# Sorted token rows packed without gaps for the expert layers, and the second pool's choices made in two parts

## What is computed

```python
x = x + 0.5 * ffn(layernorm(x))
x = x + attn(layernorm(x), Wqkv, Wo)      # 16 heads, 4 key-value heads, head size 128, causal, rotary
x = x + 0.5 * ffn(layernorm(x))

def ffn(x):                               # 16 experts, 2 per token, inner size 96
    probs = softmax(x @ router_w)
    weight, chosen = top_k(probs, 2)      # weights are normalised to a sum of 1
    return sum over the two of weight * (silu(x @ gate_w[e]) * (x @ up_w[e])) @ down_w[e]
```

## Time and profile before

| | us |
|---|---|
| median of 3 runs | 955.19 |
| lowest and highest | 954.72, 957.5 |
| the profiled execution | 958.23 |
| its span, first to last instruction | 956.3 |
| PE busy | 814.0 (85%) |
| DVE busy | 641.9 (67%) |
| ACT busy | 573.4 (60%) |
| POOL busy | 449.6 (47%) |

### The profile page before, as it was taken

One profiled execution on the slowest core, in us unless ns is written; L12 is line 12 of the kernel. 1 busy time (PEld: TensorE's weight loads), 2 busy tenths in 40 slices (PEclk: granted clock), 3 DMA queues, 4 the chain that ended last, 5 costly groups with the idle time before them and its releaser, 6 DMA issues.

```text
span 956.3 us, 16375 instructions
## 1 busy us (share of the span) xinstructions
PE 814.0 (85%) x4840; PEld 686.8 (72%) x4840; DVE 641.9 (67%) x1519; ACT 573.4 (60%) x1536; POOL 449.6 (47%) x410
## 2 busy tenths in 40 slices
PE   4457989898999999999999999999987938989490
PEld 3446878677878788787888887787776737778370
DVE  6403665467887778787877887868789735654163
ACT  3124765676677777776877876886755624445140
POOL 1472142387485756753644653643435560030623
PEclk9977999999999999999999999999999988999785
DMA  9975994211001101000000000000000452366544
GB/s 346 343 219 168 266 248 122 78 23 23 6 12 18 23 1 22 13 1 1 2 1 1 1 2 1 2 1 6 2 1 1 177 154 63 106 199 178 154 150 153
DMA packets 53812, 78.60 MB, mean 82 GB/s; under 512 B 7648, under 2 KB 44512, under 8 KB 52576
## 3 DMA queue, kind: packets, MB, share of 16 engines
q1 hardware_dynamic: 41632, 55.50, 18.1%
q0 software_dynamic: 9216, 16.82, 7.2%
q10 hardware_dynamic: 2880, 5.24, 1.9%
HBM read 42.61 MB, written 34.93 MB: 81 GB/s over the span
## 4 chain that ended last, share of the span: by engine, by line
PE 50%; issue 17%; POOL 13%; DVE 8%; ACT 4%; DMA 3%; SPq 3%; another core or an unknown queue 2%; ACTq 0%; DVEq 0%; POOLq 0%
PE ps L1593 41%; PE ps L1787 4%; POOL sb_x L1529 3%; POOL sb_ropeB L1538 3%; POOL sb_xf L1541 3%; PE ps L1647 2%; POOL sb_wF L1549 1%; DMA sb_x<-ys,sb_pos 1%; POOL xs L1511 1%; PE ps L1659 1%; DVE sb_x L1401 1%; DVE sb_wF L1381 1%; DVE sb_nmax L1374 1%; POOL xs L1504 1%
## 5 line engine op out<-in xcount | busy, mean ns | idle before, releaser
L1593 PE MATMUL ps<-sb_wF 128*128 128x512 f32 (+2 forms) x1056 | 280.0, 387 | 21.6 <-DVE sb_wF L1381 8.9
L1593 PEld LDWEIGHTS ps<-sb_wF 128*128 128x128 f32 x1056 | 170.6, 192 | 35.9 <-DVE sb_wF L1381 11.9
L1538 POOL TENSOR_TENSOR sb_ropeB<-sb_ropeB,sb_sin 128x512 f32<-128x512 f32 x80 | 109.0, 1362 | 146.0 <-ACT sb_ropeB L941 146.0
L961 ACT ACTIVATE sb_prob<-ps,sb_nmax 128x128 f32<-128x128 f32 (+3 forms) x256 | 134.5, 527 | 59.1 <-DVE sb_nmax L1374 57.1
L1593 PE MATMUL ps<-sb_wF,sb_wA 128*128 128x512 f32 x576 | 156.6, 407 | 7.6 <-ACT sb_ropeB L941 6.3
L1374 DVE TENSOR_REDUCE sb_nmax<-ps 128x1 f32<-128x128 f32 (+3 forms) x256 | 122.3, 485 | 49.8 <-PE ps L1593 45.3
L1401 DVE SCALAR_TENSOR_TENSOR sb_x<-ps,sb_rinv,sb_x 128x256 f32<-128x256 f32 x256 | 122.7, 479 | 27.4 <-PE ps L1593 11.6
L1549 POOL TENSOR_TENSOR sb_wF<-sb_xf,sb_wF 128x384 fp32r<-128x384 f32 (+1 forms) x75 | 85.5, 1141 | 114.6 <-ACT sb_wF L953 114.6
L1381 DVE TENSOR_TENSOR sb_wF<-ps,sb_wF 128x512 fp32r<-128x512 f32 x160 | 109.5, 684 | 35.0 <-ACT sb_wF L970 32.3
L1593 PE MATMUL ps<-sb_wA,sb_wF 128*128 128x256 f32 x768 | 117.5, 290 | 12.8 <-DVE sb_x L1401 8.7
L970 ACT ACTIVATE sb_wF<-ps 128x512 fp32r<-128x512 f32 x160 | 95.6, 598 | 50.0 <-PE ps L1787 37.9
(11 more groups left out here) (176 smaller groups left out, 1336.3 us busy)
## 6 DMA issues: line engine op xcount, KB each, us to landing
ys<-sb_wA_raw SPq DMA_DIRECT2D x124, 128.0 KB
xs<-sb_wA_raw SPq DMA_DIRECT2D x6, 1024.0 KB, 11.2
sb_wF_raw<-xs SPq DMA_DIRECT2D x44, 128.5 KB
sb_wA_raw<-xs SPq DMA_DIRECT2D x44, 128.5 KB
sb_work<-xs SPq DMA_DIRECT2D x36, 128.5 KB
sb_wA_raw<-in_wattn ACTq DMA_DIRECT2D x18, 256.0 KB, 3.9
sb_wF_raw<-in_wgu SPq DMA_DIRECT2D x4, 768.0 KB
sb_wF_raw<-in_wdn SPq DMA_DIRECT2D x4, 768.0 KB
```

Source lines behind the costliest of these rows:

```text
L961: nc.scalar.activation(prob[k % 2][:, h, 0:(i + 1) * P], ps[:, bank_of((k * G + h) % (UB * G)), 0:(i + 1) * P], ACT.Exp, bias=nmax[:, k % ...
L1538: nc.gpsimd.tensor_tensor(ropeB[:, slot], ropeB[:, slot], sin[:], ALU.mult).then_inc(rope_mul, 1)
L1593: return nc.tensor.matmul(out, lhsT, rhs, start=start, stop=stop)
```

## The change

The rows of the sorted tables are packed without gaps: a pair's row goes to (rows of the experts before) + rank. The tiles stay as they were, 62 in a layer and one expert each. A tile now begins at a row that is worked out on DVE: first row of its expert + 128 times its number within the expert, at most `pairs`, behind which lie 128 rows of zeros. A tile's last rows can be those of the next expert; their results go to padded places of `ys` that nothing gathers. So there are two sets of places, `to` for the scatters and `pos`, in the padded result, for the gathers. SP reads the first row of each tile into a register for each load. The zero fill of the tables goes, but for those 128 rows of each.

`places` gets five parts: counts, their sum and the first rows (0), the place of each pair (1), `to` (2), the tile tables `tab` and `begin` (3), and `pos` (4). For pools 0 and 1 the parts follow each other, all ahead of the tile loop. For pool 2 parts 3 and 4 are steps 27 and 28 of `third`; for pool 3 they stand beside tiles 21 and 22. Pool 1's choices are made in two parts, its first 8 token tiles and then its last 4; the logits of the first part go to another bank of PSUM, which PE's second tile uses later.

```diff
-    xs = [nc.dram_tensor(f"xs{n}", (pools[n].ns * P, RW), F32) for n in range(2)]
+    xs = [nc.dram_tensor(f"xs{n}", (pools[n].pairs + P, RW), F32) for n in range(2)]
...
+    FIRST_HALVES = 4
...
-                2: [(0.02, 0.4, range(18, 25)), (0.7, 0.85, range(26, 28))]},
+                2: [(0.02, 0.4, range(18, 25)), (0.7, 0.9, range(26, 29))]},
...
-        def zero_tiles(n):
-            rows = xs[n][:].rearrange("(p r) d -> p (r d)", p=P)
-            for at, width in zero_parts(n):
-                sp.dma_start(rows[:, at:at + width], zeros(width)).then_inc(zero_out[n], 16)
+        def zero_rows(n):
+            end = pools[n].pairs
+            sp.dma_start(xs[n][end:end + P, :], zeros()).then_inc(zero_out[n], 16)
...
         def load_tile(q, s):
             at = q.tiles + s
             if s == 0:
+                sp.wait_ge(begin_done, q.p + 1)
+            first = nc.values_load(begin[s:s + 1, q.p:q.p + 1], engines=[mybir.EngineType.SP], min_val=0, max_val=q.pairs,
...
+            if s == 0:
                 sp.wait_ge(scattered[q.p], 16 * q.nt)
+                if q.n == 0:
+                    sp.wait_ge(zero_out[q.p], 16)
             if at >= XR:
                 sp.wait_ge(y_evac, at - XR + 1)
-            sp.dma_start(tile_at(q, at), xs[q.p][s * P:(s + 1) * P, :]).then_inc(xg_in[at % XR], 16)
+            sp.dma_start(tile_at(q, at), xs[q.p][bass.ds(first, P), :]).then_inc(xg_in[at % XR], 16)
...
             if part == 0:
                 dve.wait_ge(rank_done, q.p + 1)
-                link(nc.vector.tensor_scalar(r["exi"][:, 0], counts_at(q), float(P - 1), None, ALU.add))
-                link(nc.vector.tensor_scalar(r["exi"][:, 1], r["exi"][:, 0], 7, None, ALU.logical_shift_right))
-                link(nc.vector.tensor_copy(te, r["exi"][:, 1]))
+                link(nc.vector.tensor_copy(count, counts_at(q)))
+                link(nc.vector.tensor_tensor_scan(end, count, count, 0.0, ALU.add, ALU.max))
+                link(nc.vector.tensor_tensor(first, end, count, ALU.subtract))
             elif part == 1:
-                link(nc.vector.tensor_tensor_scan(end, te, te, 0.0, ALU.add, ALU.max))
-                link(nc.vector.tensor_tensor(base, end, te, ALU.subtract))
...
             elif part == 2:
...
+                nc.vector.tensor_copy(r["to"][:, :, at:at + q.nt], r["pf"][:, :, 0:q.nt]).then_inc(to_done, 1)
+            elif part == 3:
+                link(nc.vector.tensor_scalar(r["exi"][:, 0], count, float(P - 1), None, ALU.add))
+                link(nc.vector.tensor_scalar(r["exi"][:, 1], r["exi"][:, 0], 7, None, ALU.logical_shift_right))
+                link(nc.vector.tensor_copy(te, r["exi"][:, 1]))
+                link(nc.vector.tensor_tensor_scan(end, te, te, 0.0, ALU.add, ALU.max))
+                link(nc.vector.tensor_tensor(base, end, te, ALU.subtract))
+                link(nc.vector.tensor_scalar(scratch, end, slot_index(q), None, ALU.is_le))
+                link(nc.vector.tensor_reduce(r["cnt"][:, 0:1], scratch, AX_X, ALU.add))
+                nc.vector.tensor_scalar(tab[:, q.p:q.p + 1], r["cnt"][:, 0:1], float(E - 1), None, ALU.min)\
+                  .then_inc(tab_done, 1)
+                link(nc.vector.scalar_tensor_tensor(back, base, -float(P), first, ALU.mult, ALU.add))
+                link(nc.vector.scalar_tensor_tensor(scratch, base, slot_index(q), back, ALU.is_le, ALU.mult))
+                link(nc.vector.tensor_reduce(r["cnt"][:, 1:2], scratch, AX_X, ALU.min))
+                link(nc.vector.scalar_tensor_tensor(r["cnt"][:, 1:2], slot_index(q), float(P), r["cnt"][:, 1:2], ALU.mult,
+                                                    ALU.add))
+                nc.vector.tensor_scalar(begin[:, q.p:q.p + 1], r["cnt"][:, 1:2], float(q.pairs), None, ALU.min)\
+                  .then_inc(begin_done, 1)
             else:
+                for k in range(2):
+                    moved = per_token(q, "lm", 2)
+                    link(nc.vector.tensor_tensor(plane(q, 1), plane(q, 2 + k),
+                                                 back.rearrange("p (o e) -> p o e", o=1).broadcast_to([P, q.nt, E]),
+                                                 ALU.mult))
+                    link(nc.vector.tensor_reduce(moved, plane(q, 1), AX_X, ALU.add))
+                    link(nc.vector.tensor_tensor(r["pf"][:, k, 0:q.nt], r["pf"][:, k, 0:q.nt], moved, ALU.subtract))
                 nc.vector.tensor_copy(pos[:, :, q.t0:q.t0 + q.nt], r["pf"][:, :, 0:q.nt]).then_inc(pos_done, 1)
...
-        nc.vector.memset(zeros(4 * 512), 0.0).then_inc(zero_set, 1)
+        nc.vector.memset(zeros(), 0.0).then_inc(zero_set, 1)
...
+        def second_choices(first, last):
+            lcopy(pools[1], first // 2)
+            chosen[1] = (first, last)
+            for part in range(6):
+                route(pools[1], part)
+            del chosen[1]
...
+        second_choices(0, 2 * FIRST_HALVES)
+        second_choices(2 * FIRST_HALVES, pools[1].nt)
+        route(pools[1], 6)
+        shares(pools[1])
+        for part in range(5):
+            places(pools[1], part)
...
-                pool.wait_ge(pos_done, q.p + 1)
-                if q.n == 0:
-                    pool.wait_ge(zero_out[q.p], 16 * len(zero_parts(q.p)))
-                else:
+                pool.wait_ge(to_done, q.p + 1)
+                if q.n == 1:
                     pool.wait_ge(xt_ps, NFIRST)
...
             if j == gathers_of(q)[0]:
+                pool.wait_ge(pos_done, q.p + 1)
...
         def gate_up(q, s, e):
             pe.wait_ge(xt_done, s + 1)
+            if s == 1:
+                pe.wait_ge(lcopy_done, copies(pools[1], 0))
```

More of the change, by code:

```diff
@@ L28, in __init__ @@
         self.nh = self.nt // 2
+        self.pairs = 2 * self.nt * P
         self.tokens = n * z.N + self.t0
@@ L448, in a0_row, with zeros @@
         return xf[:].rearrange("p k s -> p (k s)")[:, t * D:(t + 1) * D]
-    def zeros(width):
-        return wA_flat[:, 24 * 512:24 * 512 + width]
+    def zeros():
+        return wA_flat[:, 24 * 512:24 * 512 + RW]
     ROUTE = [O, O, C, O]
@@ L515, in logits_at @@
             return ps[:, third_bank(h), 0:2 * E]
-        return ps[:, LOGBANKS[q.p], 2 * h * E:2 * (h + halves) * E]
+        bank = GUBANKS[1] if q.p == 1 and h < FIRST_HALVES else LOGBANKS[q.p]
+        return ps[:, bank, 2 * h * E:2 * (h + halves) * E]
     def ranks_at(q):
@@ L750, in load_tile @@
             if s == 0:
+                sp.wait_ge(begin_done, q.p + 1)
+            first = nc.values_load(begin[s:s + 1, q.p:q.p + 1], engines=[mybir.EngineType.SP], min_val=0, max_val=q.pairs,
+                                   skip_runtime_bounds_check_because="the table holds the least of that and a place")
+            if s == 0:
                 sp.wait_ge(scattered[q.p], 16 * q.nt)
+                if q.n == 0:
+                    sp.wait_ge(zero_out[q.p], 16)
             if at >= XR:
                 sp.wait_ge(y_evac, at - XR + 1)
-            sp.dma_start(tile_at(q, at), xs[q.p][s * P:(s + 1) * P, :]).then_inc(xg_in[at % XR], 16)
+            sp.dma_start(tile_at(q, at), xs[q.p][bass.ds(first, P), :]).then_inc(xg_in[at % XR], 16)
         def store_tile(q, s):
@@ L1146, in places @@
             r = ROUTE[q.p]
-            te, end, base = r["ex"][:, 0], r["ex"][:, 1], r["ex"][:, 2]
+            te, end, base, scratch, count, first, back = (r["ex"][:, i] for i in range(7))
             place = r["L"][:, 0:q.nt * E]
@@ L1319, in third @@
             else:
-                places(q, 3)
+                places(q, n - 24)
         def early_norm(b, n):
@@ L1461, in _ @@
         sort_norm(pools[1])
-        for q in pools[0:2]:
-            lcopy(q, 0)
-            for part in range(7):
-                if q.p == 0 and part == 3:
-                    second_norm()
-                route(q, part)
-            shares(q)
-            for part in range(4):
-                places(q, part)
+        def second_choices(first, last):
[4 more added lines that the diff above has]
+            del chosen[1]
+        lcopy(pools[0], 0)
+        for part in range(7):
+            if part == 3:
+                second_norm()
+            route(pools[0], part)
+        shares(pools[0])
+        for part in range(5):
+            places(pools[0], part)
+        second_choices(0, 2 * FIRST_HALVES)
+        second_choices(2 * FIRST_HALVES, pools[1].nt)
+        route(pools[1], 6)
+        shares(pools[1])
+        for part in range(5):
+            places(pools[1], part)
         experts(0)
```

36 lines of the change are left out of this document (18 added, 18 removed).

## The result

| | before | changed |
|---|---|---|
| median, 20 runs each (us) | 954.23 | 958.6 |
| the profiled execution (us) | 958.23 | 959.92 |
| its span (us) | 956.3 | 958.1 |

The ratio of the two is 1.0047, 95% interval 1.0031 to 1.0064: some 4.5 us slower. The runs of the experiments were made on five other chips. The kernel before has medians of 953 to 960 us on three of them and of 897.5 and 899.3 us on two.

A forecast was written before the change was run, and what follows sets the result against it. Full DMA queues, then DVE's routing were taken to bound the start, and PE the tile loops. Start -5.6, last batch +2.4 and pool 3 +2.1 gave -1.1 from 955.19, so 954.1 us, range 945 to 961.

The forecast's parts named there:

- the bound for no change: Whole kernel: changes under 0.3%, 2.9 us, were to be called no change.
- rival C: Slower, 16%: DVE's new steps in the last batch outweigh the start; -2.8 + 5.4 + 3.0 = +5.6, 960.8 us.
- Zero fill: Start: eight zero-fill DMAs become two small ones, so the first tile load comes at 39.2 instead of 46.88.
- division: Start, DVE: pool 1's choices in two parts end at 37.7 instead of 39.2, 1.5 us gained.
- places at the start: DVE: pool 1's scatters from 43.8, but added place steps of 5.0 us set the first turned product at 48.2.
- The slow stretch: PE's slow tiles beside pool 1's scatters: tied to POOL 6.0 us of gain arrive, to PE's progress 2.8; taken 5.6.
- SP: Tile loop: register loads and address arithmetic for 124 loads stay hidden by ten buffers and 0.36 of slack, no cost.
- The last batch: Pool 2's routing on DVE in the attention's last groups: added steps cost 2.4 us, between 0.3 and 5.4.
- Pool 3: Second expert layer: place steps on DVE between tiles cost PE 2.1 us, bounds 0.5 and 3.0.

The follow-up runs named there:

- e14: The kernel before itself, unchanged, profiled on the same slower chip as the changed kernel's second profile; 955.45 us in one run.
- e16: The changed kernel itself, run again on a chip of the slower kind; ratio to the kernel before 1.0054.
- e7: Changed kernel with only layer 0 packed; layer 1 padded, its zero blocks written directly behind layer 0's last stores; ratio to the kernel before 0.9978.
- e13: Changed kernel with pool 1's first scatter held until its padded places are there; ratio to the kernel before 1.0063.
- e8: Changed kernel with part 4 moved: pool 1's between tiles of layer 0, pool 2's between tiles of layer 1; ratio to the kernel before 1.0045.
- e12: The changed kernel itself, run again on a chip of the faster kind; ratio to the kernel before 1.0080.
- e2: Changed kernel with only layer 1 packed; layer 0 padded, with whole zero fill and pool 1's choices undivided; ratio to the kernel before 1.0104.
- e3: Changed kernel with pool 1's choices made in one part again; ratio to the kernel before 1.0080.
- e4: Changed kernel with the whole zero fill back, pool 0's and 1's scatters waiting for it; ratio to the kernel before 1.0093.
- e5: Changed kernel with 56 waits, all met long before, added on PE ahead of its tile loop; ratio to the kernel before 1.0062.

## Why the prediction was wrong

I forecast no change, 954.1, with the sum -5.6 + 2.4 + 2.1. Measured is 958.6, slower by 4.4: inside my range, but beyond the bound for no change. It is the side and nearly the size of rival C, 960.8, to which I gave 16%.

- **Zero fill, division, places at the start**: each step right. Load 39.2 forecast, 39.13 found; scatters 43.8 and 43.90; first turned product 48.2 and 48.11, and DVE ended it. The 13 small steps and two pairs took 4.8 us, forecast 5.0.
- **The slow stretch** failed, and it is the larger miss: "Because it ended with POOL, I take 5.6." Its end did move by about 2 us with POOL, but its start moved by 5.6 with the tiles, so the tiles that start earlier fall into it. The lead behind it is 3.1 us, and 2.7 between e14 and e16; e7 gives 2.1 for all of layer 0. I had both ends, 2.8 and 6.0, and took the wrong one. What sets the start of the stretch stays open: by e13 it isn't only how far PE has come. I had also not looked past the stretch: pool 1's loads need the scatters' end, and that moved by 1.9 us only. On the faster kind of chip PE does wait there.
- **SP**: right. The loop keeps PE at 26.00 of 26. SP's new register load, from the lines of the changed kernel (minimum, median, maximum in ns):

```profile
L756 SPq TENSOR_LOAD <-sb_begin x124: 263/273/855, 28.1 to 922.2; - x124
```

  The median is 0.27 us, not the some 600 ns of the Trainium skill (DMA: Bandwidth & Descriptors, Latency and other measured facts). By that page SP would have been just full; the measurement decides.
- **The last batch** failed too: 2.4 forecast, 3.9 found in the changed kernel's profile and 3.8 to 5.2 in six others. The bounds 0.3 and 5.4 held it, but I interpolated on DVE's busy share of a whole group. The row that decides is one wait: PE was already idle for 2.75 us behind DVE's x_add at 742.37. Work that slips ahead of that x_add is paid nearly in full (2.35 of the 2.6 us of step 27, and the cast's 0.65), and the `SHARES` line of the diff moved step 27 ahead of it. I priced that step's work and not its place, and the lower clock behind the longer wait (0.9 us) not at all. The wide products kept their price (1.28 and 1.22 us here); part 4's products ran while POOL was idle and cost 0.35 us each, so the added work was 3.6 and not 5.4.
- **Pool 3**: nearly right. 2.1 forecast, 2.3 found, in the changed kernel's profile and in seven others. 1.52 of it is one idle time of PE behind DVE's tables. PE of the changed kernel:

```profile
852.39 0.69 PE L1637 MATMUL ps<-sb_wF_raw,sb_hT 96*128 x2 [1.52 <-issue]
```

With the measured terms the sum is -2.1 + 3.9 + 2.3 = 4.1, beside 4.4 measured. Of the 5.2 us between this sum and the forecast's, 3.5 are the slow stretch, 1.5 the last batch and 0.2 pool 3. That it comes so near to 4.4 is in part luck: the -2.1 has an interval of -3.8 to -0.4. Rival C had the right side for the right reason, DVE's steps in the last batch, but with 5.4 for them and 3.0 for pool 3.

## What to carry to other kernels

When a list of steps with shares of a stretch gets one entry more, the other entries move too. Print the new order and look for each operation that another engine is already waiting for: a step that slipped ahead of it here cost nearly its whole length, and with the steps spread over stretches where DVE had idle time the same work cost nothing that shows. Moving one step is not enough by itself: in e8 the wait grew by 0.65 us only, and the lower clock behind it took 2.1. And before an earlier start is counted as time, look for the next thing that it must wait for, here the second pool's scatters, and how much earlier that one comes.

## What was not expected

**Two kinds of chip.** Between 52 and 76 us, beside the scatters, the same program begins 3 down products, one for each tile, on one chip and 14 on another (PE busy for 8.66 and 22.55 us in the windows above). On the slower one the hand-overs between engines are late. ACT in the changed kernel, where PE's products were done by 52.2:

```profile
53.85 0.25 ACT L879 ACTIVATE sb_sg<-ps 128x96 f32<-128x96 f32 x1 [3.66 <-remote]
55.29 0.38 ACT L875 ACTIVATE sb_xT<-ps 128x256 f32<-128x256 f32 x1 [1.19 <-remote]
56.73 0.27 ACT L885 ACTIVATE sb_hT<-ps 96x128 f32<-96x128 f32 x1 [1.05 <-remote]
```

They are 1.44 us apart, about the pace of POOL's scatters (24 from 43.90 to 76.22, 1.35 each). In the second half of the program there are long idle times too, beside runs of POOL's indirect DMAs: in the kernel before 4.1 and 8.9 us that end at 774.7 and 789.1, and 6.9 and 6.4 that end at 900.0 and 909.5. In e12, on the faster chip, PE has none over 2.5 us at these places. Why, was not found out; PE's instruction fetch it is not. The changed kernel stood at 1.0047 and 1.0054 on two of the slower chips and at 1.0080 on a faster one, but the intervals overlap, so that its worth depends on the chip is not shown.

**A stall that also costs the clock.** Behind PE's idle time of 5.76 us the granted clock in the changed kernel was 0.64 over the next 5 us, that is for a good part at the lower of its two levels, and the six matmuls took 1.62 us instead of 0.94. PE of the changed kernel, columns as above:

```profile
743.00:748.00 5.00, 4.60 (x19) 4.04 (x20) 4.50 (x14) 3.65 (x8) 1.29 (x2) 0.64 0.00 0
```

Of the 3.9 us lost there 3.0 are the longer wait and the rest is this. Behind the wait of 2.75 us in the kernel before the granted clock was 1.00. In e8 the wait was only 3.40 us and the clock fell as well, to 0.50 (1.62 for the same matmuls), which cost more, 2.1 us. In six more profiles with a wait of 5.76 us, e2, e3, e4, e5, e13 and e16, it was 0.50 to 0.69 over the 5 us behind it, and cost 0.8 to 2.2 us.
